# Result stores and x loads of a recurrent kernel issued by GpSimd in place of SyncE

## What is computed

```
x = x + conv(x, cond_2048[:, None, :], b)        # per channel, padding (K-1, 0), K = 128
def cell(h, x):                                   # GRU, one call for each of 64 time steps
    gi = x @ W_ih + b_ih                          # [128, 512] @ [512, 1536]
    gh = h @ W_hh + b_hh
    r, z = sigmoid(i_r + h_r), sigmoid(i_z + h_z)
    n = tanh(i_n + r * h_n)
    return (1 - z) * n + z * h
x = x + scan(cell, cond_2048, x)
```

## Time and profile before

| | |
|---|---|
| times of 3 runs | 1239.12, 1239.37, 1244.23 us, median 1239.37 |
| profiled execution | span 1237.5 us from its first to its last instruction; no other time of that execution is given |
| PE | 1182.9 us busy, 96% of the span, 5518 matmuls |
| DVE, ACT, POOL | 539.3, 500.2 and 17.2 us busy |
| DMA | 97.98 MB, queue 1 (SP) 96.29 MB |

### The profile page before, as it was taken

The page is one execution under the profiler, slowest core; times in us unless marked ns, Lnnn a source line. Parts: engine busy times, 40 slices in busy tenths (PEclk is TensorE's granted clock), DMA queues, the critical chain, the costliest instruction groups (busy, mean ns, idle before and its releaser), DMA issues.

```text
span 1237.5 us, 15341 instructions
## 1 busy us (share of the span) xinstructions
PE 1182.9 (96%) x5518; PEld 986.4 (80%) x5518; DVE 539.3 (44%) x811; ACT 500.2 (40%) x934; POOL 17.2 (1%) x19
## 2 busy tenths in 40 slices
PE   1997999899989999999999999999999999999997
PEld 1976788787878888888888888888888888888886
DVE  2835766476655333333333333333333333333333
ACT  4436766576755333323333323333332333332332
POOL 0400000000000000000000000000000000000000
PEclk9999999899989999999999999999999999999999
DMA  9978888788853111111011111001111101111100
GB/s 244 293 176 161 167 173 175 170 183 174 173 149 77 54 32 35 34 34 32 24 29 34 34 34 34 25 25 34 34 34 34 28 24 34 34 34 34 32 17 21
DMA packets 288354, 97.98 MB, mean 79 GB/s; under 512 B 212752, under 2 KB 282384, under 8 KB 286272
## 3 DMA queue, kind: packets, MB, share of 16 engines
q1 hardware_dynamic: 283968, 96.29, 33.1%
q10 hardware_dynamic: 4352, 1.25, 0.4%
HBM read 63.34 MB, written 34.14 MB: 79 GB/s over the span
## 4 chain that ended last, share of the span: by engine, by line
PE 89%; ACT 3%; issue 2%; SPq 2%; DMA 2%; DVE 2%; ACTq 0%; DVEq 0%
PE bank L779 80%; PE bank L801 4%; PE bank L741 2%; PE bank L768 2%; SPq L347 1%; ACT tmp L561 1%; ACT x_parts L551 1%; SPq L358 1%; DMA early<-early_result 1%; ACT bank L519 0%; ACT toep_early L500 0%; DMA xres<-stage 0%; DVE stage L679 0%; DVE x_parts L668 0%; DMA tap_pad<-tap_rows 0%
## 5 line engine op out<-in xcount | busy, mean ns | idle before, releaser
L779 PE MATMUL bank<-w_ih_hi,xT_hi 128*128 128x512 f32 x768 | 308.2, 401 | 0.0
L779 PE MATMUL bank<-w_ih_hi,xT_lo 128*128 128x512 f32 x768 | 302.2, 394 | 0.0
L779 PE MATMUL bank<-w_ih_lo,xT_hi 128*128 128x512 f32 x768 | 302.2, 393 | 0.0
L779 PE MATMUL bank<-w_hh_hi,hT_hi 128*128 128x512 f32 x768 | 299.6, 390 | 0.0
L779 PE MATMUL bank<-w_hh_lo,hT_hi 128*128 128x512 f32 x768 | 299.5, 390 | 0.0
L779 PE MATMUL bank<-w_hh_hi,hT_lo 128*128 128x512 f32 x768 | 298.8, 389 | 0.0
L779 PEld LDWEIGHTS bank<-w_ih_hi,xT_lo 128*128 128x128 f32 x768 | 145.6, 190 | 31.8
L779 PEld LDWEIGHTS bank<-w_hh_hi,hT_lo 128*128 128x128 f32 x768 | 144.2, 188 | 30.4
L779 PEld LDWEIGHTS bank<-w_ih_hi,xT_hi 128*128 128x128 f32 x768 | 146.1, 190 | 27.2 <-ACT bank L519 0.4
L779 PEld LDWEIGHTS bank<-w_ih_lo,xT_hi 128*128 128x128 f32 x768 | 146.1, 190 | 26.8
L779 PEld LDWEIGHTS bank<-w_hh_hi,hT_hi 128*128 128x128 f32 x768 | 144.4, 188 | 28.1
(11 more groups left out here) (59 smaller groups left out, 802.3 us busy)
## 6 DMA issues: line engine op xcount, KB each, us to landing
x_unit<-in_x_dram SPq DMA_DIRECT2D x64, 256.0 KB, 4.7
toep_ring<-kernel_parts SPq DMA_DIRECT2D x128, 128.0 KB, 3.3
out_dram<-outZ SPq DMA_DIRECT2D x256, 64.0 KB, 1.6
xres<-stage SPq DMA_DIRECT2D x32, 384.0 KB, 5.0
xT<-xres SPq DMA_DIRECT2D x192, 64.0 KB, 1.9
early<-early_result SPq DMA_DIRECT2D x4, 1024.0 KB, 13.8
xT<-early SPq DMA_DIRECT2D x60, 64.0 KB, 2.0
w_ih_raw<-in_L_cond_W_ih_dram SPq DMA_DIRECT2D x12, 256.0 KB, 7.8
```

The lines of the kernel that those rows point to most:

```text
L779: mm = nc.tensor.matmul(psum[:, :], a[:, rows], b[w][:, cols], start=False, stop=stop and n == 2, skip_group_check=True)
```

## The change

The change moves three things from SP's stream to POOL's: the stores of the result (`store_out`), and the loads of the xT tiles (`load_early_xT` and `load_xT`), 508 DMAs in all (256 stores, 60 early loads, 192 later loads). The functions are the same, with `pool` for `sp`. What gates them moves too: the wait for the four `early_stored`, the wait for `outZ_ready` at each step's end, the wait for `stage_stored` after step 13, and the last wait for `out_stored`. SP keeps the loads of `x_unit` and `toep_ring` and the stores of `stage`.

```diff
@@ block.sync
-            for n in range(QUARTERS):
-                sp.wait_ge(early_stored[n], 16)
-            load_early_xT(1)
             sp.wait_ge(early_done, NB0)
             sp.wait_ge(toep_cleared, 1)
             sp.wait_ge(k_parts_stored, 16 * QUADS)
@@
-            load_early_xT(2)
-            load_early_xT(3)
@@
             def step(i, u):
                 t = i * RING + u
                 for point in range(POINTS):
                     bulk(t, point)
-                sp.wait_ge(outZ_ready, t + 1)
-                store_out(u, t)
...
-            rounds(sp, step)
-            for n in range(2):
-                sp.wait_ge(out_stored[n], 16 * QUADS * T // 2)
+                if isinstance(t, int) and t == BULK_LAST:
+                    store_stage(NBANK * 2 // STAGE - 1)
+
+            for i in range(PEELED):
+                for u in range(RING):
+                    step(i, u)
@@ block.gpsimd
             nc.gpsimd.memset(toep_ring[:, :].bitcast(F32), 0.0).then_inc(toep_cleared, 1)
+
+            for n in range(QUARTERS):
+                pool.wait_ge(early_stored[n], 16)
+            def store_out(u, t):
+                for q4 in range(QUADS):
+                    pool.dma_start(
+                        out[:, bass.ds(t, 1), :].rearrange("(Q s) o (q e) -> q s Q (o e)", s=QUAD, e=P)[q4],
+                        outZ[u % 2][q4 * QUAD:(q4 + 1) * QUAD, :].rearrange("s (Q e) -> s Q e", e=P),
+                    ).then_inc(out_stored[u % 2], 16)
+            def step(i, u):
+                t = i * RING + u
+                pool.wait_ge(outZ_ready, t + 1)
+                store_out(u, t)
+                if isinstance(t, int):
+                    if t + RING < EARLY:
+                        load_early_xT(t + RING)
+                    if t == BULK_LAST:
+                        for n in range(2):
+                            pool.wait_ge(stage_stored[n], 32 * (PAIRS // STAGE // 2))
+                        for late in range(EARLY, t + RING + 1):
+                            load_xT(late % RING, T - 1 - late)
+                    if t > BULK_LAST and t + RING < T:
+                        load_xT(u, T - 1 - RING - t)
+                else:
+                    load_xT(u, T - 1 - RING - u - i * RING)
+
+            for t in range(1, RING):
+                load_early_xT(t)
+            rounds(pool, step)
```

More of the change, by code:

```diff
@@ L326, in _ @@
                              quarter[n][:, :]).then_inc(early_stored[n], 16)
[L328 to L341, removed]
             def load_x_quarter(unit, b4):
@@ L400, in bulk @@
                     load_x_quarter(unit, b4)
[L402 to L407, removed]
             def step(i, u):
@@ L458, in _, with load_early_xT, load_xT @@
             nc.gpsimd.memset(toep_ring[:, :].bitcast(F32), 0.0).then_inc(toep_cleared, 1)
+            for n in range(QUARTERS):
+                pool.wait_ge(early_stored[n], 16)
+            def load_early_xT(t):
+                for q4 in range(QUADS):
+                    pool.dma_start(
+                        xT[t % RING][q4 * QUAD:(q4 + 1) * QUAD, :].rearrange("r (k b) -> r k b", b=B),
+                        early.rearrange("(q u h) (l r) b -> q u r (h l) b", q=QUADS, u=EARLY, r=QUAD)[
+                            q4, EARLY - 1 - t],
+                    ).then_inc(xT_loaded[t % RING], 16)
+            def load_xT(u, back):
+                for half in range(QUADS):
+                    pool.dma_start(
+                        xT[u][half * QUAD:(half + 1) * QUAD, :].rearrange("p (k b) -> p k b", b=B),
+                        xres[bass.ds(back, 1), :, :].rearrange("o (k q p) b -> q p (o k) b", p=QUAD, q=QUADS)[half],
+                    ).then_inc(xT_loaded[u], 16)
+            def store_out(u, t):
+                for q4 in range(QUADS):
+                    pool.dma_start(
+                        out[:, bass.ds(t, 1), :].rearrange("(Q s) o (q e) -> q s Q (o e)", s=QUAD, e=P)[q4],
[20 more added lines that the diff above has]
+            rounds(pool, step)
+            for n in range(2):
+                pool.wait_ge(out_stored[n], 16 * QUADS * T // 2)
         @block.scalar
```

## The result

The changed kernel takes 1208.76 us (median of 4 runs, 1208.04 to 1209.24), the kernel before 1239.86 us beside it. The ratio is 0.9756, 95% interval 0.9736 to 0.9776: 2.4% faster, where 1.9% was forecast. The profiled execution has a span of 1207.0 us, 30.5 us less than before.

The account below looks back on a forecast made before the run. Late toep_ring loads stalling PE in the bulk stage were taken as the bound. 1237.5 - 30.3 + 1.8 + 3.3 + 1.0 = 1213.3 us of span, plus 1.9 for the median: 1215.2 us, range 1206 to 1225.

Parts of the forecast that it names:

- What bounds the kernel: Bulk stage: PE stalls on late toep_ring loads and the low clock afterwards lose 31.8 us; late steps lose nothing.
- Part 1: Bulk stage: SP sheds 5.7 us of issuing a step and its place behind outZ_ready, removing stalls: -30.3 us.
- Part 2: POOL's cost p for each DMA issue: taken as 1.27 us, between 0.43 and 1.9; hidden in late steps, cost 0.
- Part 3: Step 0: step 1's xT tile lands 4p - 1.7 us later through POOL, p being its issue cost; PE stalls +1.8 us.
- Part 4: Kernel end: the last four result stores take longer to issue on POOL than on SP: +3.3 us.
- Part 5: Bulk stage: POOL's issuing lengthens DVE's operations beside it, mostly covered by DVE's idle time: +1 us.
- C: Bulk steps: DVE held up by POOL, 3.2 us a step, half uncovered: +20 us, 1235; chance 0.04.
- D: Bulk steps: POOL's issues stand still while DVE is busy, 11 us come on the path: 1226; chance 0.04.
- Rival A: Bulk stage: DMA engines set the pace, so toep_ring loads land later and stalls stay: 1225 to 1243; chance 0.17.
- Rival B: Late steps: POOL becomes the bound if an issue costs over 2.1 us; near 1370 at 2.5 us; chance 0.07.

Follow-up runs that it names:

- experiment 1: Kernel before with everything still on SyncE; in bulk steps the outZ wait and 8 DMAs moved behind point 2 of the next step: 1231.68 us, ratio 0.9940.
- 3: Kernel before with only the bulk steps' result stores moved to POOL; xT loads and late steps stay on SP: 1220.32 us, ratio 0.9852.
- 4: Kernel before with only the bulk steps' xT loads, first three tiles included, moved to POOL; stores and late steps stay on SP: 1216.70 us, ratio 0.9820.
- Experiment 2: Changed kernel with only the wait for outZ_ready put back on SyncE at each bulk step's end: 1209.11 us, ratio 0.9764.
- once more: Changed kernel run again unaltered, as the measure for a later group of runs: 1208.40 us, ratio 0.9750.
- experiment 11: Changed kernel with each late xT tile loaded by 32 DMAs of 4 partitions, 36 DMAs a step on POOL: 1796.69 us, one run.

## Why the prediction came out as it did

*What bounds the kernel.* Right: the bulk stage had lost 31.8 us to late loads of `toep_ring`, and the late steps nothing. The shape of the loss was right as well: stall and low clock afterwards both went, and the granted clock is 1.00 from step 0 to step 13.

*Part 1, SyncE's gain.* The term of -30.3 us measured -32.7. That is 0.9 us beyond its bound of -31.8, because 283.0 us for 13 steps was too long: between the transposes of steps 0 and 1 lie only 20.8 us, with 8 banks in between and not ten. The 1.5 us that I kept for step 1, as something that no earlier load helps, didn't stay: that step fell from 24.9 to 20.8 us. It stays long in versions 1 and 3 (24.6 and 25.2 us), where SP's order at the start is the old one, and is short in 4 (20.8), where it is the new one; so earlier loads are just what helped there. The reason given for the whole term held only in part. It named the 5.7 us of issuing in a step, read off one step, where all 12 together give 4.9 us a step, and "the place behind `outZ_ready`". Experiment 2 shows the place behind the wait to be free, and experiment 1 shows that the place behind the DMAs is a quarter of the gain. The rest came from taking the issues off SP's stream, and with them the DMAs off its queue.

*Part 2, an issue on POOL.* Mis-sized: p was taken at 1.27 us and measured 0.55 (0.69 with the small pauses, as 8 take 5.5 us in a late step). It was nearer to the row of SP's issue (0.43) than to a piece of POOL's own work. The 1 us of the Trainium skill that the prediction set beside p is a time to the first byte, not the time for which an issue holds POOL, and could not stand for it. That it is hidden in the late steps was right.

*Part 3, step 0.* +1.8 us forecast, +1.0 measured, by other parts than the formula's. The tile came 2.3 us later (72.14 in place of 69.83), and 4p - 1.7 with p = 0.55 gives 0.5. The fourth of the issues ended at some 69.3 us, so the landing took 2.8 us in place of 1.5. The loads of `x_unit` now run at that time; that they are the reason is not shown. PE stalled some 0.3 us for the bias behind it; the rest of the 1.0 us was not traced. The executions differ by as much: with the start as before the transposes of step 0 stand at 79.98, 80.62 (1) and 79.96 us (3), with the start of the changed kernel at 81.02, 80.68 (once more) and 80.64 us (2).

*Part 4, the end.* +3.3 us forecast, +1.2 measured; 4p - 1.8 gives 0.4 for p = 0.55. The rest is 0.3 us from outZ to the first issue and a slower landing.

*Part 5 and rivals C and D.* +1 us forecast, nothing seen. DVE's splits of x take 1106 ns before and 1110 after, its evictions 422 and 420 (medians in the bulk stage). POOL's issues of xT take 548 ns by the median in both stages, and 688 at most in the bulk stage and 567 in the late one. The Trainium skill has the rule that GpSimd can't write descriptors while DVE runs in a fast two-port mode ("SBUF — State Buffer", "SBUF: two separate sides"). Nothing of the kind is seen here, but no run shows in which mode DVE's operations are, so this neither bears the rule out nor contradicts it.

*Rival A.* Wrong as a bound: the loads of toep_ring land in 3.5 us where they took 3.3, and x_unit in 5.0 for 4.7, though the same loads now come in 260 us in place of 293, and some 13 us (6 banks) lie between release and use. The Trainium skill says that a second issuing engine only saves the time of the issue, and that this is usually small beside the DMA itself ("DMA: Bandwidth & Descriptors", "Issuing engines are not separate DMA queues"). The first half agrees with the runs as far as they go. The second holds here too (0.45 us of issue for a store that lands in 1.8 us in the bulk stage, medians); but the gain near 0 that the prediction drew from it doesn't follow, for what counts is the sum of the issues on one stream and not one issue beside its DMA.

*Rival B.* Not met at 8 DMAs a step, and real at 36 (experiment 11). Its point of crossing, 8p = 16.8, leaves out the pauses.

*Luck.* None was needed for the number: all four terms erred to the slow side (by 2.4, 0.8, 2.1 and 1.0 us), and together they are the 6.3 us between 1213.3 and the span of 1207.0. A p more than twice too large cost little, because only the start and the end have it on the path.

## What to carry to other kernels

Before you argue about the place of a DMA in a queue, add up for how long the issuing engine's stream is occupied over the stage, and set it against the stage's length at full pace. Here nothing was lost at 222 of 260 us (85%) and 10 us at 233 (90%); what it would be in another kernel is not shown. Don't expect to gain the moved issues' own time: 58.6 us left SP's stream in the stretch and 32.7 us were gained, for the gain ends where PE no longer waits. Nor need all of them move: from step 1 on, either half gave two thirds of the gain. The same DMAs at another place in the same stream gave a quarter of it, and on an engine with work of its own a half.

## What the runs showed of the hardware

- A DMA of 64 KB in runs of 512 B is 32 packets when POOL issues it (16256 for 508), and 144 when SP does: queue 1 fell from 283968 to 210816 packets for the same 508.
- POOL's issue of such a DMA takes 0.55 us, and in late steps it lands in 1.9 us (stores) and 2.1 us (loads), in place of 1.6 and 1.9 from SP, whose issue takes 0.32 us there. The Trainium skill puts the first byte at some 1 us for GpSimd against 0.6 us for SyncE ("DMA: Bandwidth & Descriptors", "Latency and other measured facts"); the difference here has the same sign.
- In the bulk stage, on a queue beside SP's, landing took 3.1 and 3.4 us in place of 1.8 and 2.0 on SP's own. From ACT it took 3.1 and 3.4 us as well, so this is not a matter of POOL.
- With 1024 bytes a partition of room POOL issued seven such DMAs and paused: 1.5 us at 71 us, until 0.3 us after the first xT tile was used, and 5.7 us at 111 us, where a store took 7.5 us to land. With 2048 it issued twelve without a pause.
- DMAs of 64 bytes between device memories, eight to a step, went with loads beside them that landed up to 12.2 us after issue (median 4.7), where the changed kernel has 6.8 (median 3.5).
